# First layer of a graph kernel: one-hot comparisons that read the column numbers from a PSUM bank, and a sort whose ranks use one bank

## Chip, cores and metric

The kernel runs on one core of a Trainium2 chip. The metric is device time in microseconds of one execution. Before the change it is 9839.95 us, the median of three executions (9836.8 to 9844.66 us).

## What is computed

The reference runs two graph layers over 6,250 nodes with 128 features and 206,250 directed edges. Only the first layer and a sort for the second one matter here.

```python
msg = edge_weight[:, None] * x[src]                       # first layer
agg = segment_sum(msg, dst, num_segments=N)
out = relu((x + agg) @ W1 + b1) @ W2 + b2
x = layernorm(x + out)
# second layer, three hops: attention over the edges of each head
# (head = src), softmax per head, weighted sum of rel * agg[tail]
```

The second layer needs the edges grouped by `src`, the order in which it walks its heads. That sort depends on the indices alone, and the kernel does it while the first layer's gather runs.

## The kernel before

**The stage.** Edges are handled in tiles of 128 (one edge to a partition), four tiles to a group (`GROUP` = 4), and there are 1,664 tiles in 416 groups. All engines walk the same list of steps, each in a program order of its own, and meet at semaphores. Step i works on different groups in different functions; a "lag" says how many steps behind the newest group a function is. The stage is one block of the program (L1229 to L1251), in which each engine has one function that it calls at every step.

**First layer's part.** GpSimd (`pool_rows`, L602) issues one indirect DMA for each tile, which gathers 128 rows of `x` by their source index. The ring holds four groups of rows. ScalarE multiplies each tile by its edge weights (L1211) and copies the indices of later groups (L629). VectorE builds `hot`, a one-hot matrix for each tile, by comparing the row of numbers 0 to 127 (`column`, in SBUF) with each edge's target number (L1193). TensorE multiplies one by the other into bank 0 or 1 (L1223). VectorE then adds the result to `acc` (L1190).

**The sort's part.** A counting sort of the edges by source node rides along, with the same groups, in blocks of 32 groups (`IN_BLOCK`). VectorE makes two one-hots of each tile (`vector_tag`: `of_section` L1012, `of_low` L1014). TensorE sums them (`tensor_sum`, L1026 and L1028). 37 steps later (`RANK`) TensorE turns them into ranks (`tensor_rank`, L1095 and L1096, written to bank 4 or 5 in turn), and VectorE picks each edge's own rank (`vector_own` L1102, `vector_spot` L1110). 69 steps after the tag (`LAY`) the edges are laid out by two more one-hots: one on VectorE (`in_row` L1133, then two products `paid` L1141), one on ScalarE (`apart` L1152, `in_column` L1156). TensorE multiplies these two into bank 6 (`tensor_lay`, L1167). At a block's end there is extra work: `vector_totals`, `tensor_ahead`, `vector_carry`, a round trip through memory for the carries (SyncE, L1074 and L1078), and `vector_where`.

**Order within one step.** VectorE: add the group of three steps ago to `acc`, build `hot`, [`vector_where`], `own`, `in_row`, `spot`, `paid` twice, `of_section`, `of_low`, [totals, carry]. TensorE: L1223 for the group of two steps ago, rank, sum, [ahead], lay. ScalarE: weigh, copy indices, [laid], `apart` four times, `in_column`. GpSimd does nothing but issue gathers. The functions in brackets run once in 32 steps.

**What waits for what.** `hot` of step i waits for TensorE's L1223 of the same step i, since it has two buffers. `own` of step i stands behind it in VectorE's queue, and waits for the rank of TensorE's step i-1. In TensorE's step i the rank waits for `spot` of VectorE's step i-1:

```python
s.wait_ge((s_spot, done(lag + 2)))     # tensor_rank, L1094
```

Four of VectorE's operations at every step take `column` as one operand, and a second tensor in SBUF as the other: L1193, L1012, L1014 and L1133. `own` and the additions to `acc` take one operand from PSUM. `paid` takes both from SBUF.

Of the kernel before, what the change touches and what calls it, by code (L numbers as in the profile page):

```python
# [6 lines left out]
ALU = mybir.AluOpType  # L7
# [8 lines left out]
P = 128  # L16
BANK = 512
GROUP = BANK // P
# [102 lines left out]
def done(lag, per=1):  # L121
    return lambda i: per * (i - lag + 1) if i >= lag else 0
# [23 lines left out]
def phases(e, name, step, groups, total, rates, unroll=UNROLL):  # L146

    regs = {rate: e.alloc_register(f"{name}_rate{rate}") for rate in rates}
    spare = [e.alloc_register(f"{name}_until{n}") for n in range(8)]
    for start in range(0, total, IN_BLOCK):  # L150
        whole = start + IN_BLOCK <= total
        for i in range(start, start + 2 * unroll if whole else total):
            step(Step(e, i, groups))
        if whole:
            turns = IN_BLOCK // unroll - 2
            for rate in rates:
                e.reg_mov(regs[rate], rate)
            with e.Fori(0, turns) as turn:
                for b in range(unroll):
                    step(Step(e, start + 2 * unroll + b, groups, turn, regs, spare, unroll, turns))  # L160
                for rate in rates:
                    e.reg_add(regs[rate], regs[rate], rate)
    for r in [*regs.values(), *spare]:
        e.free_register(r)


def gnn_two_layers(nc, x, src, dst, edge_type, edge_weight, w1, b1, w2, b2, edge_emb, q_w, k_w, out):
# [3 lines left out]
    with top:  # L171
        def sem(name):
            return Sem(top.enter_context(nc.semaphore(name)))

        def tensor(ctx, name, shape, dt=F32):
            return ctx.enter_context(nc.sbuf_tensor(name, shape, dt))
# [5 lines left out]
        bank = [banks_used[:, i, :] for i in range(8)]  # L182
# [8 lines left out]
        H = P // 2  # L191
# [4 lines left out]
        column = tensor(top, "column", [P, P])  # L196
# [441 lines left out]
        S = z.sections  # L638
# [5 lines left out]
        with ExitStack() as ctx:  # L644
# [5 lines left out]
            above_half = tensor(ctx, "above_half", [P, P], BF16)  # L650
            ones_short = tensor(ctx, "ones_short", [P, P], BF16)
            two = tensor(ctx, "two", [2, P], BF16)
# [65 lines left out]
            with ExitStack() as tmp:  # L718
                start = tensor(tmp, "start", [H, 2])
# [241 lines left out]
            hot = tensor(inner, "l0_hot", [P, 2, GROUP, P])  # L961
# [3 lines left out]
            of_section = tensor(inner, "of_section", [P, IN * GROUP * S], BF16)  # L965
            of_low = tensor(inner, "of_low", [P, 2, GROUP, P], BF16)
            carry_rows = tensor(inner, "carry_rows", [2, IN * GROUP * S], BF16)
# [5 lines left out]
            own = tensor(inner, "own", [P, 2, GROUP, S])  # L973
# [5 lines left out]
            in_row = tensor(inner, "in_row", [P, GROUP, H], F16)  # L979
# [5 lines left out]
            s_carry, s_split, s_carried, s_rank, s_own, s_spot = (sem(f"sort_s_{n}") for n in ("carry", "split", "carried", "rank", "own", "spot"))  # L985
            s_where, s_in_row, s_paid, s_apart = (sem(f"sort_s_{n}") for n in ("where", "in_row", "paid", "apart"))
            s_in_column, s_laid, s_lain, s_blocks = (sem(f"sort_s_{n}") for n in ("in_column", "laid", "lain", "blocks"))
            s_carries = [sem(f"sort_s_carries{i}") for i in range(2)]
            b_totals, b_rank, b_laid, b_heads = 2, 4, 6, 7
            TAG, RANK, LAY = 0, IN_BLOCK + 5, IN + 5  # L990
            steps = z.sort_groups + LAY + 3
            paid_words = pay[:, :, :].bitcast(F16)
# [6 lines left out]
            def tagged(s, lag):  # L999
                return of_section[:, ring_at(s, lag, S)].rearrange("p (t s) -> p t s", s=S)  # L1000
# [6 lines left out]
            def vector_tag(s):  # L1007
                e = s.e
                if s.live(TAG, z.sort_groups):
                    cols = bass.ds(s.at(lambda i: GROUP * i), GROUP)  # L1010
                    s.wait_ge((s_summed, done(2)), (s_spot, done(IN)))
                    e.scalar_tensor_tensor(tagged(s, TAG), column[:, 0:S].unsqueeze(1).to_broadcast([P, GROUP, S]), 1.0,  # L1012
                                           sec_of[:, cols].unsqueeze(2).to_broadcast([P, GROUP, S]), ALU.mult, ALU.is_equal)
                    e.scalar_tensor_tensor(of_low[:, s.slot(TAG, 2), :, :], column[:, :].unsqueeze(1).to_broadcast([P, GROUP, P]), 1.0,  # L1014
                                           head_low[:, cols].unsqueeze(2).to_broadcast([P, GROUP, P]), ALU.mult, ALU.is_equal).then_inc(s_tagged.h, 1)

            def tensor_sum(s):
# [69 lines left out]
            def tensor_rank(s):  # L1087
                e, lag = s.e, RANK - 1
                if s.live(lag, z.sort_groups):
                    k, g2 = s.block(lag), s.slot(lag, 2)  # L1090
                    if s.begins_block(lag):
                        e.wait_ge(s_carries[k % 2].h, 16 * (k // 2 + 1))
                    s.wait_ge((s_spot, done(lag + 2)))
                    cols = ring_at(s, lag, S)  # L1094
                    e.matmul(bank[b_rank + g2][:, 0:GROUP * S], above_half[:, :], of_section[:, cols], start=True, stop=False)  # L1095
                    e.matmul(bank[b_rank + g2][:, 0:GROUP * S], two[:, :], carry_rows[:, cols], start=False, stop=True).then_inc(s_rank.h, 1)  # L1096

            def vector_own(s):
                if s.live(RANK, z.sort_groups):
                    g2 = s.slot(RANK, 2)  # L1100
                    s.wait_ge((s_rank, done(RANK)), (s_spot, done(RANK + 2)))
                    s.e.tensor_tensor(own[:, g2, :, :], bank[b_rank + g2][:, 0:GROUP * S].rearrange("p (t s) -> p t s", s=S), tagged(s, RANK), ALU.mult)\  # L1102
                        .then_inc(s_own.h, 1)

            def vector_spot(s):
# [24 lines left out]
            def vector_in_row(s):  # L1130
                if s.live(LAY, z.sort_groups):
                    s.wait_ge((s_paid, done(LAY + 1)))
                    s.e.scalar_tensor_tensor(in_row[:, :, :], column[:, 0:H].unsqueeze(1).to_broadcast([P, GROUP, H]), 1.0,  # L1133
                                             spot_row[:, ring_at(s, LAY)].unsqueeze(2).to_broadcast([P, GROUP, H]), ALU.mult, ALU.is_equal).then_inc(s_in_row.h, 1)

            def vector_paid(s):
# [44 lines left out]
            def vector_l0(s):  # L1181
                e = s.e
                if s.live(3):
                    q = load_sections(s, mybir.EngineType.DVE, at_wide, (z.sections - 1) * WIDE, 3)
                    s.wait_ge((s_acc, done(3)), (s_taken, lambda i: GROUP * (i - 3)))
                    for t in range(GROUP):
                        if t:
                            s.wait_ge((s_taken, lambda i, t=t: GROUP * (i - 3) + t))
                        to = acc[:, bass.ds(q[t], P)]
                        e.tensor_tensor(to, to, bank[s.slot(3, 2)][:, t * P:t * P + P], ALU.add).then_inc(s_taken.h, 1)  # L1190
                if s.live(0):
                    s.wait_ge((s_acc, done(2)))
                    e.scalar_tensor_tensor(hot[:, s.slot(0, 2), :, :], column[:, :].unsqueeze(1).to_broadcast([P, GROUP, P]), 1.0,  # L1193
                                           low_of[:, bass.ds(s.at(lambda i: GROUP * i), GROUP)].unsqueeze(2).to_broadcast([P, GROUP, P]),
                                           ALU.mult, ALU.is_equal).then_inc(s_l0_hot.h, 1)
                vector_where(s)
                vector_own(s)
                vector_in_row(s)
                vector_spot(s)
                vector_paid(s)  # L1200
                vector_tag(s)
                vector_totals(s)
                vector_carry(s)
# [26 lines left out]
            with nc.Block() as block:  # L1230
                @block.sync
                def _(e):
                    sync_sort(e)

                @block.gpsimd
                def _(e):
                    pool_rows(e, "l0", rows, idx, x, s_rt)

                @block.scalar
                def _(e):  # L1240
                    phases(e, "ga", scalar_l0, z.slot_groups, steps, (UNROLL, 16 * GROUP))

                @block.vector
                def _(e):
                    e.memset(counts[:, :], 0.0)
                    phases(e, "gv", vector_l0, z.slot_groups, steps, (UNROLL, GROUP * UNROLL))
                    e.wait_ge(s_taken.h, z.slot_tiles)

                @block.tensor
                def _(e):  # L1250
                    phases(e, "gt", tensor_l0, z.slot_groups, steps, (UNROLL, GROUP * UNROLL))  # L1251
# [674 lines left out]
```

## Time and profile before

| what | value |
|---|---|
| median of three executions | 9839.95 us |
| the profiled execution's own time | 9834.6 us |
| its span in the profile | 9832.9 us |
| busy: TensorE, VectorE, ScalarE, GpSimd | 7328.8, 6365.0, 5947.2, 6751.4 us |
| gathers of the first layer: number, busy | 1664, 1707.7 us |
| first and last of them start at | 346.9 and 2560.7 us |

Busy time is that of the instructions themselves. Times inside the profile are counted from the span's start. The stage that the diff touches lies between about 346 and 2788 us. The table's busy shares cover the whole kernel, so the stage has to be read by itself. GpSimd's instruction for a gather is the making of the DMA's descriptors; the transfer follows it.

### The profile page before, as it was taken

How to read it: one execution, taken by the hardware profiler on the slowest of the kernel's cores; microseconds unless marked ns; L12 is line 12 of the kernel's file. 1: busy time of each engine (PE TensorE's matmuls, PEld its weight loads, DVE VectorE, ACT ScalarE, POOL GpSimd, SP SyncE). 2: the span in 40 equal slices, each digit the busy share in tenths (PEclk: the TensorE clock that was granted, in tenths of full speed). 3: DMA queues.
4: the chain of work that ended last, by engine and by line, in shares of the span. 5: the costliest groups of instructions: out<-in, count | busy, mean ns of one | idle time of the engine just before them, and what ended most of it. 6: DMA issues, size and time to landing. Idle time of an engine off the chain costs nothing. (4 is left out here: it accounts for less than half of the span.)

```text
span 9832.9 us, 248228 instructions
## 1 busy us (share of the span) xinstructions
PE 7328.8 (75%) x47197; PEld 5463.0 (56%) x47197; DVE 6365.0 (65%) x27494; ACT 5947.2 (60%) x15127; POOL 6751.4 (69%) x6760
## 2 busy tenths in 40 slices
PE   0357777777749999999996777777776777777774
PEld 0345555555536777777764555555554555555553
DVE  2368877877656777777765666666665656666566
ACT  1137777777846666666664666666664666666663
POOL 0677777777327777777764777777774777777773
PEclk9657777777559999999998999999998999999997
DMA  1111211112217777777785666666665666666664
GB/s 45 40 50 50 51 50 50 51 50 50 22 35 213 222 224 222 223 224 223 223 209 140 176 175 176 176 175 176 175 176 124 173 174 174 175 173 174 172 175 103
DMA packets 1389939, 1398.93 MB, mean 142 GB/s; under 512 B 239111, under 2 KB 1066274, under 8 KB 1389602
## 3 DMA queue, kind: packets, MB, share of 16 engines
q1 hardware_dynamic: 1173096, 951.41, 31.9%
q0 software_dynamic: 215904, 443.45, 19.4%
q10 hardware_dynamic: 804, 2.56, 0.1%
q8 instruction: 50, 0.82, 0.0%
q14 instruction: 85, 0.70, 0.0%
HBM read 888.05 MB, written 183.75 MB: 109 GB/s over the span
## 5 line engine op out<-in xcount | busy, mean ns | idle before, releaser
L602 POOL DMA_INDIRECT tails<-node_rows,idx x4992 | 4925.2, 987 | 1866.6 <-issue 1516.0
L1655 DVE SCALAR_TENSOR_TENSOR acc<-acc,fade,banks 128x129 f32 x4992 | 1721.1, 345 | 1092.5 <-PE banks L1743 688.2
L602 POOL DMA_INDIRECT l_rows<-in_x_dram,l_idx x1664 | 1707.7, 1026 | 531.2 <-issue 500.9
L1743 PE MATMUL banks<-rt,weight_t 128*128 128x129 f32 x9984 | 1427.5, 286 | 804.4 <-DVE acc L1655 781.0
L1743 PEld LDWEIGHTS banks<-rt,weight_t 128*128 128x128 f32 x9984 | 1223.6, 192 | 1061.7 <-issue 1050.3
L1767 ACT ACTIVATE weight<-att,low 128x128 f32<-128x128 f32 x4992 | 1593.9, 395 | 344.5 <-DVE low L1694 342.1
L1751 ACT ACTIVATE weight_t<-banks 128x512 f32<-128x512 f32 x1248 | 746.3, 598 | 1570.2 <-PE banks L1730 1024.2
L1723 PE MATMUL banks<-right,window 128*128 128x128 f32 x9984 | 1391.0, 283 | 0.2 <-DVE tile_low L1661 0.2
L1661 DVE CUSTOM_DVE_ANT_0 att<-banks,mask 128x128 f32<-128x128 f32 x4992 | 1235.9, 285 | 103.6 <-PE banks L1723 100.5
L1734 PE MATMUL banks<-rtt,k_sb 128*128 128x512 f32 x2496 | 1288.1, 598 | 1.4 <-ACT rtt L1758 1.4
L1723 PEld LDWEIGHTS banks<-right,window 128*128 128x128 f32 x9984 | 1241.0, 195 | 28.2 <-DVE tile_low L1661 0.4
L1738 PEld LDWEIGHTS banks<-ident,rt 128*128 128x128 f32 x4992 | 569.5, 142 | 1175.4 <-DVE rt L1676 876.6
L1676 DVE SCALAR_TENSOR_TENSOR rt<-rel,tails 128x512 f32<-128x512 f32 x832 | 576.6, 693 | 967.8 <-DMA tails<-node_rows,idx 938.4
L1223 PE MATMUL banks<-l_weighed,l_hot 128*128 128x128 f32 x3328 | 723.0, 386 | 431.5 <-issue 399.2
L1738 PE MATMUL banks<-ident,rt 128*128 128x128 f32 x4992 | 795.1, 282 | 294.8 <-DVE rt L1676 284.2
L1754 ACT ACTIVATE right<-banks 128x512 f32<-128x512 f32 x1248 | 745.9, 598 | 343.6 <-PE banks L1734 295.0
L1223 PEld LDWEIGHTS banks<-l_weighed,l_hot 128*128 128x128 f32 x3328 | 628.4, 282 | 548.9 <-issue 533.2
L1211 ACT ACTIVATE l_weighed<-l_rows,l_weights 128x128 f32<-128x128 f32 x1664 | 531.5, 390 | 637.3 <-DMA l_rows<-in_x_dram,l_idx 637.3
L1758 ACT ACTIVATE rtt<-banks 128x512 f32<-128x512 f32 x1248 | 741.8, 594 | 277.3 <-PE banks L1738 270.3
L1167 PE MATMUL banks<-in_column,paid 128*64 128x256 f16 x3328 | 645.7, 360 | 268.6 <-ACT in_column L1156 221.7
L1730 PE MATMUL banks<-ident,weight 128*128 128x128 f32 x4992 | 761.2, 276 | 3.5 <-ACT weight L1767 2.4
L1152 ACT ACTIVATE apart<-spread,spot_left 128x256 f32<-128x256 f32 x1664 | 705.7, 494 | 18.7 <-DVE spot_left L1127 3.5
(293 smaller groups left out, 9300.8 us busy)
## 6 DMA issues: line engine op xcount, KB each, us to landing
window<-qt SPq DMA_DIRECT2D x4992, 64.0 KB
rel<-rel_kept SPq DMA_DIRECT2D x832, 256.0 KB
rows_in<-tile_rows SPq DMA_DIRECT2D x416, 256.0 KB
rel_kept<-rel SPq DMA_DIRECT2D x416, 256.0 KB
mask<-mask_kept SPq DMA_DIRECT2D x832, 128.0 KB
tails<-node_rows,idx POOLq DMA_INDIRECT x4992
mask_kept<-mask SPq DMA_DIRECT2D x416, 128.0 KB
l_rows<-in_x_dram,l_idx POOLq DMA_INDIRECT x1664
```

Source lines behind the costliest of these rows:

```text
L602: e.indirect_dma_start(out=rows[:, g, t % GROUP, :], out_offset=None, in_=of, in_offset=bass.IndirectOffsetOnAxis(ap=idx[:, b, t:t + 1], a ...
L1223: mm = s.e.matmul(bank[g2][:, t * P:t * P + P], hot[:, g2, t, :], weighed[:, g2, t, :], start=True, stop=True)
L1655: e.scalar_tensor_tensor(to, to, fade[:, g2, t:t + 1], bank[b_acc + t // 2][:, t % 2 * WIDE:t % 2 * WIDE + WIDE], ALU.mult, ALU.add).then_ ...
L1661: e.tensor_tensor_reduce(att[:, g2, t, :], bank[b_att][:, t * P:t * P + P], mask[:, g4, t, :], 1.0, START, ALU.add, ALU.min, tile_low[:, g ...
L1723: mm = e.matmul(bank[b_att][:, t * P:t * P + P], window[:, g4, t, :], right[:, g2, t * P:t * P + P], start=True, stop=True)
L1730: mm = e.transpose(bank[b_et][:, t * P:t * P + P], weight[:, g2, t, :], ident[:, :])
L1734: e.matmul(bank[b_kw][:, :], k_sb[:, :], rtt[:, s.slot(2, 2), :], start=True, stop=True).then_inc(s_kw.h, 1)
L1738: mm = e.transpose(bank[b_rtt][:, t * P:t * P + P], rt[:, s.slot(1, UNROLL), t, 0:z.D], ident[:, :])
L1743: mm = e.matmul(bank[b_acc + t // 2][:, t % 2 * WIDE:t % 2 * WIDE + WIDE], weight_t[:, s.slot(4, 2), t, :], rt[:, s.slot(4, UNROLL), t, :] ...
L1751: e.activation(weight_t[:, s.slot(4, 2), :, :].rearrange("p t d -> p (t d)"), bank[b_et][:, :], ACT.Copy).then_inc(s_ets.h, 1)
L1754: e.activation(right[:, s.slot(2, 2), :], bank[b_kw][:, :], ACT.Tanh).then_inc(s_th.h, 1)
L1767: e.activation(weight[:, g2, t, :], att[:, g2, t, :], ACT.Exp, scale=-1.0, bias=low[:, g4, t + 1:t + 2]).then_inc(s_exp.h, 1)
```

## The change

The diff does three things. It copies `column` once into bank 5 before VectorE's first step. It lets the four comparisons read it from there (`from_psum`). And, since bank 5 is taken, both ranks in turn now go to bank 4. TensorE's rank therefore waits until VectorE's `own` has read the rank before it, and no longer for `spot`.

```diff
+            s_column = sem("sort_s_column")
-            b_totals, b_rank, b_laid, b_heads = 2, 4, 6, 7
+            b_totals, b_rank, b_column, b_laid, b_heads = 2, 4, 5, 6, 7
+            from_psum = bank[b_column][:, 0:P]
...
-                    e.scalar_tensor_tensor(tagged(s, TAG), column[:, 0:S].unsqueeze(1).to_broadcast([P, GROUP, S]), 1.0,
+                    e.scalar_tensor_tensor(tagged(s, TAG), from_psum[:, 0:S].unsqueeze(1).to_broadcast([P, GROUP, S]), 1.0,
...
-                    e.scalar_tensor_tensor(of_low[:, s.slot(TAG, 2), :, :], column[:, :].unsqueeze(1).to_broadcast([P, GROUP, P]), 1.0,
+                    e.scalar_tensor_tensor(of_low[:, s.slot(TAG, 2), :, :], from_psum.unsqueeze(1).to_broadcast([P, GROUP, P]), 1.0,
...
-                    s.wait_ge((s_spot, done(lag + 2)))
+                    s.wait_ge((s_own, done(lag + 1)))
                     cols = ring_at(s, lag, S)
-                    e.matmul(bank[b_rank + g2][:, 0:GROUP * S], above_half[:, :], of_section[:, cols], start=True, stop=False)
-                    e.matmul(bank[b_rank + g2][:, 0:GROUP * S], two[:, :], carry_rows[:, cols], start=False, stop=True).then_inc(s_rank.h, 1)
+                    e.matmul(bank[b_rank][:, 0:GROUP * S], above_half[:, :], of_section[:, cols], start=True, stop=False)
+                    e.matmul(bank[b_rank][:, 0:GROUP * S], two[:, :], carry_rows[:, cols], start=False, stop=True).then_inc(s_rank.h, 1)
...
-                    s.e.scalar_tensor_tensor(in_row[:, :, :], column[:, 0:H].unsqueeze(1).to_broadcast([P, GROUP, H]), 1.0,
+                    s.e.scalar_tensor_tensor(in_row[:, :, :], from_psum[:, 0:H].unsqueeze(1).to_broadcast([P, GROUP, H]), 1.0,
...
-                    e.scalar_tensor_tensor(hot[:, s.slot(0, 2), :, :], column[:, :].unsqueeze(1).to_broadcast([P, GROUP, P]), 1.0,
+                    e.scalar_tensor_tensor(hot[:, s.slot(0, 2), :, :], from_psum.unsqueeze(1).to_broadcast([P, GROUP, P]), 1.0,
...
                     e.memset(counts[:, :], 0.0)
+                    e.tensor_copy(from_psum, column[:, :]).then_inc(s_column.h, 1)
+                    e.wait_ge(s_column.h, 1)
```

## Rows read from the trace of the kernel before

**Rows 1.** The page's costliest groups: the first layer's gathers; busy, mean ns, idle before.

```profile
L602 POOL DMA_INDIRECT l_rows<-in_x_dram,l_idx x1664 | 1707.7, 1026 | 531.2 <-issue 500.9
```

**Rows 2.** Line L602 by itself: duration ns min/median/max, first and last start us.

```profile
L602 POOL DMA_INDIRECT l_rows<-in_x_dram,l_idx x1664: 941/947/1511, 346.9 to 2560.7; - x185
```

**Rows 3.** Timeline of VectorE and GpSimd: start us, us, engine, operation, idle before.

```profile
1508.74 1.54 DVE L1190 TENSOR_TENSOR acc<-acc,banks 128x128 f32 x4
...
1509.35 0.95 POOL L602 DMA_INDIRECT l_rows<-in_x_dram,l_idx  x1 [0.30 <-issue]
...
1511.70 0.69 DVE L1193 SCALAR_TENSOR_TENSOR l_hot<-column,l_low_of 128x512 f32<-128x512 f32 x1 [1.42 <-PE banks L1223]
...
1511.85 1.36 POOL L602 DMA_INDIRECT l_rows<-in_x_dram,l_idx  x1 [0.31 <-issue]
```

**Rows 4.** Windows: busy us and count by engine, TensorE's granted clock, DMA share, GB/s.

```profile
347.00:716.00 369.00, 182.00 (x1170) 154.07 (x1170) 203.94 (x561) 93.91 (x306) 284.59 (x277) 0.50 0.20 50
716.00:2565.00 1849.00, 1341.05 (x9014) 1017.53 (x9015) 1472.32 (x4282) 1447.54 (x3297) 1423.03 (x1387) 0.72 0.21 50
1278.60:1295.60 17.00, 14.48 (x79) 10.72 (x80) 12.21 (x35) 12.37 (x29) 13.04 (x14) 0.52 0.19 48
1346.90:1360.40 13.50, 6.45 (x60) 4.98 (x61) 11.81 (x36) 9.63 (x23) 10.45 (x11) 0.98 0.17 45
```

**Rows 5.** VectorE's groups by form, 716 to 2565 us: busy, mean ns, idle before.

```profile
L1193 DVE SCALAR_TENSOR_TENSOR l_hot<-column,l_low_of 128x512 f32<-128x512 f32 x346 | 239.8, 693 | 227.4 <-PE banks L1223 224.5 <-issue 1.4
...
L1102 DVE TENSOR_TENSOR own<-banks,of_section 128x196 f32<-128x196 f32 x346 | 122.4, 354 | 0.4
L1012 DVE SCALAR_TENSOR_TENSOR of_section<-column,sec_of 128x196 f32 x263 | 92.5, 352 | 0.0
```

**Rows 6.** Timeline of a step at half clock, TensorE and VectorE together.

```profile
1284.50 2.04 PE L1223 MATMUL banks<-l_weighed,l_hot 128*128 128x128 f32 x8 [1.18 <-issue]
1286.34 0.37 PE L1095 MATMUL banks<-of_section,above_half 128*128 x1
...
1286.70 0.69 DVE L1193 SCALAR_TENSOR_TENSOR l_hot<-column,l_low_of 128x512 f32<-128x512 f32 x1 [1.39 <-PE banks L1223]
...
1286.92 0.22 PE L1026 MATMUL banks<-of_section,picker 128*128 x1
...
1287.31 0.35 DVE L1102 TENSOR_TENSOR own<-banks,of_section 128x196 f32<-128x196 f32 x1
```

**Rows 7.** The rest of a step at half clock: sum, lay, and the next step's L1223.

```profile
1218.18 0.22 PE L1026 MATMUL banks<-of_section,picker 128*128 128x49 bf16 x1
...
1218.63 1.92 PE L1167 MATMUL banks<-in_column,paid 128*64 128x256 f16 x8
...
1220.47 2.08 PE L1223 MATMUL banks<-l_weighed,l_hot 128*128 128x128 f32 x8
```

**Rows 8.** Timeline of steps at full clock, TensorE and VectorE together.

```profile
1211.25 0.20 PE L1026 MATMUL banks<-of_section,picker 128*128 128x49 bf16 x1
...
1211.56 1.06 PE L1167 MATMUL banks<-in_column,paid 128*64 128x256 f16 x8
...
1354.53 1.13 PE L1223 MATMUL banks<-l_weighed,l_hot 128*128 128x128 f32 x8 [1.16 <-issue]
...
1355.50 0.25 PE L1095 MATMUL banks<-of_section,above_half 128*128 x1
...
1355.82 0.69 DVE L1193 SCALAR_TENSOR_TENSOR l_hot<-column,l_low_of 128x512 f32<-128x512 f32 x1 [0.51 <-PE banks L1223]
1355.87 0.20 PE L1026 MATMUL banks<-of_section,picker 128*128 x1
```

**Rows 9.** VectorE's timeline: two starts of L1193 with no idle time between.

```profile
1213.82 0.68 DVE L1193 SCALAR_TENSOR_TENSOR l_hot<-column,l_low_of 128x512 f32<-128x512 f32 x1
...
1218.29 0.68 DVE L1193 SCALAR_TENSOR_TENSOR l_hot<-column,l_low_of 128x512 f32<-128x512 f32 x1
```

**Rows 10.** Waits, 722 to 2480 us: us in total, times, longest us.

```profile
PE banks L1045 <- DVE totals L1037: 27.4, 10, 3.3
```

More of the change, by code:

```diff
@@ L1089, in tensor_rank @@
                 if s.live(lag, z.sort_groups):
-                    k, g2 = s.block(lag), s.slot(lag, 2)
+                    k = s.block(lag)
                     if s.begins_block(lag):
                         e.wait_ge(s_carries[k % 2].h, 16 * (k // 2 + 1))
-                    s.wait_ge((s_spot, done(lag + 2)))
+                    s.wait_ge((s_own, done(lag + 1)))
                     cols = ring_at(s, lag, S)
-                    e.matmul(bank[b_rank + g2][:, 0:GROUP * S], above_half[:, :], of_section[:, cols], start=True, stop=False)
-                    e.matmul(bank[b_rank + g2][:, 0:GROUP * S], two[:, :], carry_rows[:, cols], start=False, stop=True).then_inc(s_rank.h, 1)
+                    e.matmul(bank[b_rank][:, 0:GROUP * S], above_half[:, :], of_section[:, cols], start=True, stop=False)
+                    e.matmul(bank[b_rank][:, 0:GROUP * S], two[:, :], carry_rows[:, cols], start=False, stop=True).then_inc(s_rank.h, 1)
             def vector_own(s):
@@ L1101, in vector_own @@
                     s.wait_ge((s_rank, done(RANK)), (s_spot, done(RANK + 2)))
-                    s.e.tensor_tensor(own[:, g2, :, :], bank[b_rank + g2][:, 0:GROUP * S].rearrange("p (t s) -> p t s", s=S), tagged(s, RANK), ALU.mult)\
+                    s.e.tensor_tensor(own[:, g2, :, :], bank[b_rank][:, 0:GROUP * S].rearrange("p (t s) -> p t s", s=S), tagged(s, RANK), ALU.mult)\
                         .then_inc(s_own.h, 1)
```

## The prediction

> **What bounds the kernel now.** The page comes first. The stage of the diff has 1,664 gathers, and GpSimd is busy 1707.7 us with them and idle 531.2 us, nearly all of it put down to "issue" and not to a wait for another engine [rows 1]. Line L602 by itself gives the pace: the first starts at 346.9 us, the last at 2560.7 us, so 2213.8 / 1663 = 1.331 us from one to the next [rows 2]. The timeline shows 0.30 us between two gathers each time [rows 3], and 1.026 + 0.305 makes up that 1.331. So GpSimd never waits for data. It sets the stage's length, with 4 x 1.331 = 5.325 us per step of four tiles.
>
> The median gather takes 947 ns and the mean 1026, with a maximum of 1511 [rows 1, 2]. The timeline says what the long ones have in common. The gather that starts at 1511.85 does so inside a `hot` that ends at 1512.39, and takes 1.36 us: 0.41 more than usual, where 0.54 of `hot` was left. The gather that starts at 1509.35 does so inside the additions to `acc`, which read one operand from PSUM, and takes 0.95 [rows 3]. I read it so: a VectorE operation with both operands in SBUF holds up a gather that starts under it. All long gathers together cost 1664 x (1.026 - 0.947) = 131 us.
>
> Who is second? TensorE's granted clock is 0.50 until 716 us, where L1167 has not begun, and 0.72 on average after that, changing between half and full (1.2 and 2.4 GHz) [rows 4]. In a stretch at half clock TensorE is busy 14.48 of 17.0 us; in one at full clock 6.45 of 13.5 us [rows 4]. VectorE is idle 227.4 us before `hot`, nearly all of it waiting for L1223 [rows 5].
>
> **Part 1, four comparisons read PSUM.** What it frees lies on the bound. If all long gathers became 0.947 us, a step would be 4 x (0.947 + 0.305) = 5.01 us. `paid` keeps both operands in SBUF, and so keeps a tenth or so of the 131 us (it holds 0.75 us of a step, the four comparisons about 2 us). I take 5.04 us per step as GpSimd's floor. Over 415 steps 5.325 - 5.04 is worth 118 us; the bounds are 0 (the reading of the rows is wrong) and 131.
>
> The price of a PSUM operand on VectorE: `own` reads PSUM and takes 354 ns for 196 elements, `of_section` reads SBUF alone and takes 352 for as many [rows 5]. That is 2 ns, 8 ns for four in a step; I take zero. A gain is excluded, since the pair shows none at equal size. What no row shows is an operand in PSUM that is repeated four times over. From L1012 to L1193, 316 more elements cost 341 ns, so the 196 of `own` cost 211 of its 354 and the other 143 are fixed [rows 5]. Were each repeat to pay that anew, `hot` would take 3 x 0.143 = 0.43 us more; that is the bound from above. The Trainium skill, VectorE: DVE Perf Modes, "The TRN2 errata", gives VectorE 58 fixed cycles from SBUF and 120 from PSUM. By that page each comparison would take 62 cycles or some 65 ns more, an estimate, and a step's VectorE work 0.26 us more. The two rows show 2 ns where that page has 65.
>
> The one copy of `column` and its wait come before VectorE's first step. The nearest row is `own`, 0.35 us for more elements [rows 5]; it costs 0 to 0.4 us, and I take 0, as TensorE and ScalarE have nothing to do without the first gather.
>
> **Part 2, one bank for the ranks.** No instruction is added, but TensorE waits in a new place. In step i its rank must wait for `own` of VectorE's step i. `own` stands behind `hot`, and `hot` waits for L1223 of that same step. Before, rank followed L1223 at once (1286.34 after 1284.50) [rows 6]. Behind the waiting rank stand sum, lay and the next L1223. So one loop now runs through both engines, and its length per step is, at half clock:
> - L1223's start to `hot`'s start 2.20 (1284.50 to 1286.70); to `own`'s start 0.61 and its end 0.35; handing over about 0.06, an estimate (L1193 starts 0.16 behind L1223's end) [rows 6].
> - rank to sum 0.58 (1286.34 to 1286.92) [rows 6]; sum to lay 0.45, lay to the next L1223 1.84 [rows 7].
> - Sum 6.09 us, over today's 5.325.
>
> At full clock: 1.29 to `hot` [rows 8], 0.96 and 0.06 as before, rank to sum 0.37, sum to lay 0.31, lay about 1.03 [rows 8]; 4.02 us. But VectorE itself needs 4.47 us from one `hot` to the next [rows 9], so such a step takes 4.47.
>
> The rows ring (four groups) lets GpSimd run on while TensorE is late, so the mean counts. Of the time 0.56 is at half clock (0.72 = 1 - 0.56/2). If whole steps fall at one clock, a step takes 1 / (0.56/6.09 + 0.44/4.47) = 5.26 us. If clock changes fall evenly within steps, VectorE's limit is not felt: 1.18 us of a step do not scale (0.61 + 0.35 + 0.06 + 0.16), 2.84 us at full clock do and take 4.91 at half, so in the mix 2.84 / (0.44 + 0.56 x 2.84/4.91) = 3.71, in all 4.89 us. A block's end adds TensorE's wait for the totals, 27.4 us in 10 blocks [rows 10], or 0.09 us per step, and extra work on VectorE that I put at as much again, an estimate: up to 0.18. That makes 4.89 to 5.44. With GpSimd's floor of 5.04 beside a loop of almost the same length, I take 5.25.
>
> **The sum.** Until L1167 begins the loop is shorter even at half clock (6.09 less lay's 1.84 is 4.25), so GpSimd bounds: 69 steps x (5.35 - 5.01) = 23 us, where 369/69 = 5.35 is what they take now [rows 4]. After that 346 steps x (5.33 - 5.25) = 28 us. Together -51 us. Against the profiled execution's 9834.6 us that is 9784; the median of the runs is 5 us above it, so I say 9788.
>
> **Rivals.**
> - **The loop hides.** Slow and fast steps even out in the ring, and GpSimd's floor holds: 346 x 0.29 + 23 = 123 us, 9717. For: the even mix gives 4.89. Against: VectorE's 4.47 and the blocks' ends. Chance 0.17.
> - **The loop binds and TensorE sits at half clock longer.** TensorE's clock stayed at half through a stretch in which it was busy 14.48 of 17.0 us [rows 4], and the new wait (0.61 + 0.35 + 0.06 us and more, after each L1223) makes it idle more. At a share of 0.68, whole steps take 1 / (0.68/6.09 + 0.32/4.47) = 5.46, with 0.15 for blocks 5.61: 346 x 0.28 - 23 = +74 us, 9914. It turns to slower where a step passes 5.33 + 23/346 = 5.40 us, that is a share of 0.56 if whole steps fall at one clock, and about 0.64 halfway between the two ways of mixing. Chance 0.26, likeliest near +45.
> - **They cancel.** A step of 5.35 to 5.45: within 20 us. Chance 0.15.
> - **GpSimd is not freed.** The Trainium skill, SBUF — State Buffer, "Who interferes with whom", infers that an operation with two SBUF inputs takes only the shared read interface, and that making descriptors needs the write one. As a mechanism here: the long gathers stay as they are, and only part 2 is left; a step stays at 5.325 or becomes the loop's, 9840 to 9880. Against it stand the 1.36 us gather and the 0.95 one [rows 3]. Chance 0.04, counted as slower.
>
> **How the numbers follow.** About 0.2% (20 us) is what a measurement of this kernel can tell from no change. My forecast (a gain of 20 to 90 us) has 0.38, the full gain 0.17: faster 0.55. Same 0.15. Slower 0.26 + 0.04 = 0.30. The range runs from 9716 (the full gain) to 9900 (most of the slower cases). The forecast's own range is 9750 to 9820.
>
> **What the profile would show.** Part 1 right: L602 `l_rows` has a mean of 950 to 965 ns, and gathers that start under `hot` take 0.95; `hot` and `of_low` stay near 690. If they stay at 1026, part 1 is wrong. Part 2 right: a new wait of TensorE's L1095 for VectorE's `own` of about a microsecond per step, hundreds of us in all, and GpSimd begins to wait for ScalarE's indices in parts of the stage. If that wait is there and GpSimd still never waits, the first rival holds. A granted clock under 0.68 in the stage goes with the second. The forecast is wrong if the last gather starts before 2470 us or after 2541.

## The result, and the profile after

The changed kernel takes 9953.57 us (median of four executions, 9946.97 to 9965.68) against 9842.27 us for the kernel before in the same session. The ratio is 1.0115, with a 95% interval of 1.0098 to 1.0133. A gain was forecast, and a loss came, beyond the range given, which ended at 9900 us. The profiled execution took 9951.03 us, 116 us more than that of the kernel before.

Two groups of the page, and line L602 by itself (its columns are those of [rows 1] and [rows 2]), changed kernel:

```profile
span 9949.4 us, 248229 instructions
...
L602 POOL DMA_INDIRECT l_rows<-in_x_dram,l_idx x1664 | 1588.5, 955 | 743.8 <-issue 493.0
...
L1225 PE MATMUL banks<-l_weighed,l_hot 128*128 128x128 f32 x3328 | 772.7, 405 | 115.1 <-issue 93.0
```

```profile
L602 POOL DMA_INDIRECT tails<-node_rows,idx x4992: 942/947/1462, 3055.6 to 9828.8; - x200
L602 POOL DMA_INDIRECT l_rows<-in_x_dram,l_idx x1664: 941/947/1206, 349.3 to 2656.8; - x185
```

The first part of the change did all that it was meant to. The gathers' mean fell from 1026 to 955 ns [rows 1], and the longest from 1511 to 1206 [rows 2]. GpSimd is busy 119 us less. Yet the last gather starts at 2656.8 us instead of 2560.7, 96 us later: GpSimd's idle time grew by 213 us. From its first gather to its last the stage takes 94 us more (2307.5 us against 2213.8), and the gathers begin 2 us later. Of the other 20 us, 19 lie in the second layer, whose code is the same (see the end of the experiments).

The windows before and after L1169 (L1167 before) begins, with the columns of [rows 4], changed kernel:

```profile
349.00:696.00 347.00, 188.19 (x1160) 157.10 (x1160) 203.46 (x561) 93.93 (x306) 262.27 (x278) 0.50 0.21 53
696.00:2667.00 1971.00, 1502.94 (x9018) 1121.23 (x9018) 1463.13 (x4282) 1435.06 (x3306) 1326.24 (x1387) 0.68 0.20 47
```

The first 69 steps now take 347 us and took 369 [rows 4], 22 us less. The other 346 take 1971 and took 1849: 5.70 us a step against 5.34. The granted clock fell from 0.72 to 0.68. The waits of the stretch from 722 to 2480 us, with the columns of [rows 10], changed kernel:

```profile
ACT apart L1154 <- PE banks L1169: 408.6, 267, 3.2
PE banks L1097 <- DVE own L1104: 400.8, 308, 2.8
...
POOL l_rows L602 <- issue: 365.1, 1131, 2.1
DVE l_hot L1195 <- PE banks L1225: 323.9, 255, 2.8
POOL l_rows L602 <- ACT l_idx L629: 207.3, 108, 6.0
```

TensorE's rank (L1097) waits 400.8 us for `own`, 1.3 us each time. Behind that, ScalarE waits for TensorE's lay (L1169), and GpSimd waits for the indices that ScalarE copies (L629). GpSimd no longer sets the pace. A step at half clock, from the timeline of the changed kernel:

```profile
1282.94 0.69 DVE L1195 SCALAR_TENSOR_TENSOR l_hot<-banks,l_low_of 128x512 f32<-128x512 f32 x1 [1.47 <-PE banks L1225]
1283.55 0.35 DVE L1104 TENSOR_TENSOR own<-banks,of_section 128x196 f32<-128x196 f32 x1
...
1284.06 0.34 PE L1097 MATMUL banks<-of_section,above_half 128*128 x1 [1.27 <-DVE own L1104]
...
1284.61 0.22 PE L1028 MATMUL banks<-of_section,picker 128*128 x1
...
1285.24 1.89 PE L1169 MATMUL banks<-in_column,paid 128*64 128x256 f16 x8
...
1287.06 1.67 PE L1225 MATMUL banks<-l_weighed,l_hot 128*128 128x128 f32 x8
```

The reader sees the loop in one piece: `hot` waits for TensorE, `own` stands behind `hot`, the rank waits for `own`, and sum, lay and the next L1225 stand behind the rank. `hot` itself takes 0.69 us, as it did from SBUF [rows 3].

### The profile page after: what moved, and what is told of

It is laid out like the page before. It is cut to its first block and busy times, and to the rows that moved or that the text cites. A ratio compares the mean times of both kernels' runs of the same rounds, so it can differ in the third digit from the quotient of the medians.

```text
span 9949.4 us, 248229 instructions
## 1 busy us (share of the span) xinstructions
PE 7485.5 (75%) x47197; PEld 5548.4 (56%) x47197; DVE 6355.9 (64%) x27495; ACT 5933.8 (60%) x15127; POOL 6650.4 (67%) x6760
## 5 line engine op out<-in xcount | busy, mean ns | idle before, releaser
L602 POOL DMA_INDIRECT tails<-node_rows,idx x4992 | 4942.1, 990 | 1868.4 <-issue 1521.2
L602 POOL DMA_INDIRECT l_rows<-in_x_dram,l_idx x1664 | 1588.5, 955 | 743.8 <-issue 493.0
L1225 PE MATMUL banks<-l_weighed,l_hot 128*128 128x128 f32 x3328 | 772.7, 405 | 115.1 <-issue 93.0
L1225 PEld LDWEIGHTS banks<-l_weighed,l_hot 128*128 128x128 f32 x3328 | 667.4, 298 | 238.3 <-issue 238.2
L1169 PE MATMUL banks<-in_column,paid 128*64 128x256 f16 x3328 | 671.6, 370 | 57.0 <-ACT in_column L1158 44.7
```

What stands on the lines that cost most here:

```text
L602: e.indirect_dma_start(out=rows[:, g, t % GROUP, :], out_offset=None, in_=of, in_offset=bass.IndirectOffsetOnAxis(ap=idx[:, b, t:t + 1], a ...
L1225: mm = s.e.matmul(bank[g2][:, t * P:t * P + P], hot[:, g2, t, :], weighed[:, g2, t, :], start=True, stop=True)
```

## Experiments

The kernel before was run beside each group of kernels, on the same chip. Its own median differs by up to 0.9% from group to group (9753.88 to 9842.27 us), so ratios are compared. The times in the expectations of e1 to e4 were written with the kernel before at 9840 us; beside them it took 9797, so they are to be read some 43 us lower.

| run | what differs | median us | before us | ratio, 95% interval |
|---|---|---|---|---|
| changed kernel | | 9953.57 | 9842.27 | 1.0115 [1.0098, 1.0133] |
| e1 | part 2 alone | 9934.27 | 9797.25 | 1.0140 [1.0123, 1.0157] |
| e2 | part 1 alone | 9693.18 | 9797.25 | 0.9893 [0.9876, 0.9909] |
| e3 | changed, `own` ahead of `hot` | 9690.19 | 9797.25 | 0.9890 [0.9873, 0.9906] |
| e4 | changed, rank at the step's end | 9692.32 | 9797.25 | 0.9894 [0.9877, 0.9910] |
| e5 | changed, wait filled with 10 matmuls | 9710.00 | 9820.39 | 0.9890 [0.9874, 0.9907] |
| e6 | e3, `hot` from SBUF | 9749.86 | 9820.39 | 0.9928 [0.9912, 0.9945] |
| e7 | changed kernel again | 9935.15 | 9820.39 | 1.0116 [1.0100, 1.0133] |
| e8 | kernel before again | 9822.10 | 9820.39 | 1.0003 [0.9992, 1.0013] |
| e9 | changed, wait filled with 4 matmuls | 9683.41 | 9753.88 | 0.9924 [0.9907, 0.9940] |
| e10 | before, with the 10 matmuls | 9774.72 | 9753.88 | 1.0021 [1.0011, 1.0030] |

**The two parts, each alone.** e1 keeps the one bank and its wait and takes the column numbers from SBUF:

```diff
-            from_psum = bank[b_column][:, 0:P]
+            from_psum = column[:, :]
...
-                    e.tensor_copy(from_psum, column[:, :]).then_inc(s_column.h, 1)
-                    e.wait_ge(s_column.h, 1)
```

> Part 2 alone: ranks in one bank with the wait for own, column still read from SBUF. Theory A (the new wait closes a loop L1223-hot-own-rank-sum-lay through TensorE and VectorE, and that loop sets the step): about as slow as the changed kernel or somewhat slower, since the first 69 steps no longer gain 23 us and hot is still lengthened now and then by gathers: 9950 to 9985 us, the gathers' mean stays at 1.02 us or so, TensorE's L1097-type wait for own 400 us or more. Theory B (reading the column numbers from PSUM is what costs): 9840, as before. Theory C (the two parts cost about half each): 9890 to 9910.

e2 keeps the two banks and their old wait. The bank for the column numbers is bank 7, whose head counts move to a corner of the totals' banks:

```diff
-                        mm = e.matmul(bank[b_heads][:, 0:S], of_low[:, s.slot(lag, 2), t, :], own_column,
-                                      start=begins and k == 0 and t == 0, stop=True, skip_group_check=True)
+                        mm = e.matmul(bank[b_totals + k % 2][:, 4 * H:4 * H + S], of_low[:, s.slot(lag, 2), t, :], own_column,
+                                      start=False, stop=True, skip_group_check=True)
...
+                    e.tensor_tensor(head_counts[:, :], head_counts[:, :], bank[b_totals + k % 2][:, 4 * H:4 * H + S], ALU.add)
                     e.tensor_copy(totals[:, :], bank[b_totals + k % 2][:, 0:S]).then_inc(s_totals.h, 1)
```

> Part 1 alone: the column numbers in a bank of their own, ranks in two banks with the old wait. The bank comes from the head counts, which are summed in a corner of the totals' banks and added up once in 32 steps (one small VectorE operation, 13 in all). Theory A: the gathers' mean falls to 0.955 us, GpSimd stays the bound, a step takes 5.04 to 5.10 us in place of 5.33, so 9720 to 9750 us. Theory B: 9930 or more. Theory C: 9880 to 9900.

Part 2 alone costs 1.40% and part 1 alone gains 1.07%. The page's line of the gathers, first e1, then e2:

```profile
L602 POOL DMA_INDIRECT l_rows<-in_x_dram,l_idx x1664 | 1678.6, 1009 | 686.2 <-issue 492.8
```

```profile
L602 POOL DMA_INDIRECT l_rows<-in_x_dram,l_idx x1664 | 1590.5, 956 | 530.9 <-issue 505.2
```

In e1 the gathers stay long and GpSimd idles as well. In e2 they are short, and its idle time is what it was before, 531 us [rows 1]. Against the kernel before, e1 loses 137 us and e2 gains 104 us. So the loss comes with the new wait, and none of it from reading PSUM. Theory A holds in both, theories B and C fall. As the loop sets the pace with either kind of gather, the changed kernel keeps little of part 1: 1.15% against 1.40%, which is about the 22 us of the first 69 steps.

**The wait without the loop.** e3 moves one call of VectorE. `own` needs the rank of TensorE's step before, and nothing of this step's L1225:

```diff
                         e.tensor_tensor(to, to, bank[s.slot(3, 2)][:, t * P:t * P + P], ALU.add).then_inc(s_taken.h, 1)
+                vector_own(s)
                 if s.live(0):
                     s.wait_ge((s_acc, done(2)))
...
                 vector_where(s)
-                vector_own(s)
                 vector_in_row(s)
```

> The changed kernel with one call moved: VectorE does own ahead of hot, so that own no longer stands behind the wait for L1223 of the same step. One bank for the ranks and the column numbers from PSUM stay. Theory A: the loop is cut, TensorE's wait for own almost vanishes, GpSimd bounds again: 9715 to 9760 us, granted clock in the stage back to 0.72 or so. Theory B: no change from the changed kernel, 9950. A rival of its own: one bank costs by itself, since rank and own now alternate strictly wherever they stand: 9850 to 9950.

e4 leaves VectorE alone and moves TensorE's rank:

```diff
-                tensor_rank(s)
                 tensor_sum(s)
                 tensor_ahead(s)
                 tensor_lay(s)
+                tensor_rank(s)
```

> The changed kernel with TensorE's rank moved from behind L1223 to the end of its step, behind lay. The wait for own stays as it is, but sum and lay now run while VectorE does hot and own. Theory A: the wait is covered, 9715 to 9780 us. If the wait is only moved (own late even at the step's end, above all at full clock), 9800 to 9900. Theory B: 9950.

Both keep one bank and the new wait, and both are 1.1% faster than the kernel before and 2.2% faster than the changed one. Two of the waits of e3, from 720 to 2400 us:

```profile
POOL l_rows L602 <- issue: 403.8, 1325, 0.3
...
PE banks L1097 <- DVE own L1104: 216.9, 184, 3.8
```

That TensorE's wait for `own` would almost vanish was a miss: 216.9 us of it are left. But GpSimd's longest idle stretch is 0.3 us: the wait costs nothing, as it is no longer part of a loop longer than GpSimd's step. The rival that one bank costs by itself falls.

**How much is the clock's?** e5 puts matmuls that nobody reads into the wait:

```diff
+                if s.live(RANK - 1, z.sort_groups):
+                    for n in range(10):
+                        s.e.matmul(bank[b_heads][:, 2 * P:3 * P], before[:, :], ones_short[:, :], start=False, stop=True, skip_group_check=True)
                 tensor_rank(s)
```

> The changed kernel with ten extra 128-column bf16 matmuls in each of TensorE's steps, between L1223's group and the wait of the rank, into a corner of bank 7 that nothing reads: work that fills the wait of about 1.3 us. Theory A2 (a good part of the loss is that the wait lets the granted clock drop, which then lengthens the loop itself): the granted clock in the stage rises from 0.68 to over 0.85, the step falls towards GpSimd's 5.07 us, and the kernel becomes faster by adding work, 60 to 230 us below the changed kernel. Rival (the wait alone counts, and the clock hardly): the clock rises but the time stays within 30 us of the changed kernel's, or grows where the extra matmuls outlast the wait.

The timeline of e5, TensorE and one row of VectorE, full clock:

```profile
1285.01 0.72 PE L1229 MATMUL banks<-ones_short,before 128*128 128x128 bf16 x10
1286.43 0.26 PE L1097 MATMUL banks<-of_section,above_half 128*128 x1 [0.70 <-DVE own L1104]
...
1286.81 0.20 PE L1028 MATMUL banks<-of_section,picker 128*128 x1
...
1287.50 1.03 PE L1169 MATMUL banks<-in_column,paid 128*64 128x256 f16 x8
```

```profile
1285.94 0.35 DVE L1104 TENSOR_TENSOR own<-banks,of_section 128x196 f32<-128x196 f32 x1
```

The windows from 720 to 2400 us, with the columns of [rows 4]. The changed kernel:

```profile
720.00:2400.00 1680.00, 1281.27 (x7671) 955.95 (x7669) 1244.87 (x3645) 1218.57 (x2808) 1133.20 (x1185) 0.68 0.19 47
```

e8, the kernel before:

```profile
720.00:2400.00 1680.00, 1216.78 (x8246) 925.18 (x8246) 1347.08 (x3917) 1324.41 (x3017) 1294.44 (x1266) 0.73 0.20 51
```

e3:

```profile
720.00:2400.00 1680.00, 1297.75 (x8666) 977.45 (x8665) 1419.61 (x4114) 1389.19 (x3164) 1275.31 (x1329) 0.78 0.21 53
```

e5:

```profile
720.00:2400.00 1680.00, 1316.25 (x12072) 1042.80 (x12072) 1412.27 (x4146) 1397.55 (x3187) 1272.54 (x1338) 0.94 0.21 53
```

e9, with four matmuls (below):

```profile
720.00:2400.00 1680.00, 1279.58 (x9938) 984.06 (x9936) 1390.43 (x4095) 1379.19 (x3156) 1269.73 (x1326) 0.86 0.19 53
```

e10, the kernel before with the ten (below):

```profile
720.00:2400.00 1680.00, 1201.47 (x11473) 999.27 (x11474) 1354.27 (x3941) 1330.53 (x3031) 1292.37 (x1273) 0.89 0.18 51
```

The last count of a row, GpSimd's, is the number of gathers in 1680 us: 1185 in the changed kernel, 1266 before, 1338 in e5, although e5 keeps the whole loop and adds ten matmuls to each step. The granted clock is 0.94 and was 0.68. Rank, sum and lay wait for `own` as before, but at full clock that loop is shorter than GpSimd's step: between 720 and 2400 us GpSimd never idles longer than 0.31 us here. The gain of 2.2% over the changed kernel lies at the upper end of what theory A2 expected. So the loop is what makes the stage depend on TensorE's clock, and the low clock is what makes the loop longer than a gather's pace. In these runs either alone costs nothing.

e9 has four in place of ten.

> The changed kernel with four extra matmuls per step in the wait in place of ten, about 0.4 us of work at half clock in a wait of 1.3 us. Theory A2 (the loss is carried by the clock): a granted clock between 0.69 and 0.94 and a time between the two kernels, 9730 to 9900 us with the kernel before near 9820. Rival (something else in the ten matmuls helped, or it is all or nothing): the time of the changed kernel (1.2% over before) or that of the ten (1.1% under before).

Four suffice for a clock of 0.86 and a ratio of 0.9924, between the changed kernel and e5, and nearer to e5. e10 gives the ten to the kernel before, where GpSimd bounds.

> The kernel before (two banks, column numbers in SBUF) with the ten extra matmuls at the same place. Theory A2: the granted clock in the stage rises from 0.73 to 0.9 or more, and the time stays within 15 us, since GpSimd's gathers set the pace and not TensorE. Rival (a higher clock is worth time by itself in this stage, whatever bounds it): 30 us or more faster.

There the clock is 0.89, where e8 has 0.73, and the gathers stay at about their pace (1273 against e8's 1266). GpSimd's idle time ahead of its gathers is 530.6 us here and 531.0 in e8. So a higher clock alone gained nothing where TensorE is not in the bounding loop. The whole time rose by 0.21%, 21 us, where 15 at most were expected. Where it rose is open: e8, the profile of the kernel before that stands beside it here, is from another chip, on which that kernel takes 66 us more.

**The gathers' delay, one operation of four.** e6 is e3 with `hot` alone back on SBUF:

```diff
-                    e.scalar_tensor_tensor(hot[:, s.slot(0, 2), :, :], from_psum.unsqueeze(1).to_broadcast([P, GROUP, P]), 1.0,
+                    e.scalar_tensor_tensor(hot[:, s.slot(0, 2), :, :], column[:, :].unsqueeze(1).to_broadcast([P, GROUP, P]), 1.0,
```

> The kernel with own ahead of hot, with hot alone reading the column numbers from SBUF again; the other three comparisons stay on PSUM. Theory D (a gather that starts under a VectorE operation with two SBUF operands waits for its end): the gathers' long ones come back where they start under hot and nowhere else new, about 40 to 60 us in all, mean 0.98 us, and the kernel is 30 to 60 us slower than with own first alone. Rival (the whole gain needs all four, or comes from elsewhere): no change, or all 115 us.

Line L602 by itself, first e3, then e6:

```profile
L602 POOL DMA_INDIRECT l_rows<-in_x_dram,l_idx x1664: 938/944/1212, 343.3 to 2442.4; - x185
```

```profile
L602 POOL DMA_INDIRECT l_rows<-in_x_dram,l_idx x1664: 940/944/1460, 350.4 to 2487.7; - x185
```

The stage from first to last gather takes 2137.3 us against 2099.1: 38 us for one operation of the four. The gathers' mean is 980 ns against 957, and 1664 x 0.023 is 38 us as well. Counted from the traces by the VectorE operation under which a gather starts, 213 of the 239 gathers under `hot` take over 1 us in e6, and none of 238 in e3. The long ones under `paid` fall from 129 to 10, so 38 us is what is left of a larger delay under `hot`. So the delay follows the operation that has two operands in SBUF, and its cost reaches the end in full where GpSimd bounds. The two runs are from different chips, but their ratios agree: 0.9928 - 0.9890 is 0.38%, or 37 us.

**Again on one chip.**

> The changed kernel as it is, beside the kernel before on the same chip. First profile: the stage took 97 us more and the second layer, whose code is the same, 19 us more. If the 19 us are a matter of one execution or chip, the second layer takes what it takes in the others of this chip (within 8 us) and the ratio is 1.010 to 1.013; if the change does it, it is again 15 to 20 us longer than in the kernel before.

> The kernel before as it is, for a profile from the same chip as the others: a stage of 2,214 us from the first gather to the last, a granted clock of 0.72 in it, and the second layer within 8 us of that of the changed kernel in this call.

The ratio of e7 repeats the first, 1.0116. The second layer's gathers, first e7, then e8:

```profile
L602 POOL DMA_INDIRECT tails<-node_rows,idx x4992: 938/944/1466, 3049.9 to 9808.9; - x200
```

```profile
L602 POOL DMA_INDIRECT tails<-node_rows,idx x4992: 938/944/1464, 2955.5 to 9695.8; - x200
```

From first to last it is 6759.0 us in the changed kernel and 6740.3 in the one before, 19 us more. In the first pair of profiles it was 6773.2 and 6754.5, also 19. So it was not a matter of one execution or chip, and what e8 expected of the second layer (within 8 us) was a miss. Its instructions are the same. The page's line of the same gathers, first e7, then e8:

```profile
L602 POOL DMA_INDIRECT tails<-node_rows,idx x4992 | 4926.4, 987 | 1870.0 <-issue 1513.0
```

```profile
L602 POOL DMA_INDIRECT tails<-node_rows,idx x4992 | 4909.2, 983 | 1868.4 <-issue 1511.8
```

So 17 of the 19 us are longer gathers. Counted from the traces, they are those that start under `rt`, a VectorE operation with two operands in SBUF: 693 gathers in e7 against 647 in e8, with means of 1247 and 1244 ns, where the median gather takes 944. It is the same delay, met more often. On e7's chip, e5 has 6755.4 from first to last and e6 6738.1. What moves the gathers under `rt` is open, and it is a sixth of the loss.

## Why the prediction was wrong

- **What bounds the kernel: right.** GpSimd's gathers did, and the reading of their long ones as VectorE operations with two SBUF operands is shown by e2, e3 and e6. The floor was put at 5.04 us a step. e3's later steps, the 346 after the first 69, take 5.08 (from the starts of `hot`).
- **Part 1's price: right.** `hot` 691 ns on average against 693 [rows 5], `of_section` 354 against 352 (lines below). The estimate by the Trainium skill, VectorE: DVE Perf Modes, "The TRN2 errata", some 65 ns more each, is not seen here. The inference of the Trainium skill, SBUF — State Buffer, "Who interferes with whom", by which the gathers would have stayed long, is contradicted on one chip: with the comparisons reading SBUF (e1) the gathers' mean is 1009 ns, with PSUM (e2) it is 956.
- **The first 69 steps: right.** 23 us were expected, 22 came.
- **Part 2 at half clock: right.** 6.09 us were worked out. Counted from the trace, there are 97 steps between 720 and 2440 us that lie wholly at half clock, and they take 6.22 on average: 3.31 to the rank, 0.55 to the sum, 0.55 to lay and 1.82 to the next step. The difference is the handing over from `own`, 0.15 us (median) in place of 0.06, and sum to lay, where 0.45 was put in.
- **The mean step: this is the step that failed.** It was put at 5.25 us, and is 5.70. "If whole steps fall at one clock" gave 5.26 and "if clock changes fall evenly within steps" gave 4.89, both with the share of half clock of the kernel before, 0.56. Three things were wrong, and a middle between the two ways could not hold them.
  - The share of half clock rose to 0.64 (a granted clock of 0.68). Put into the first way, that alone gives 5.39 us.
  - Neither way of mixing is what happens. Among 299 steps counted, one lay wholly at full clock; it took 4.02 us, the loop's own sum and not VectorE's 4.47, which shows in e9 (median 4.49 of 175 such steps). 201 are mixed and take 5.49, although the clock is full for over half of their time, where the even way gives about 4.7. In these steps the granted clock is 0.76 from L1225's start to the rank, 0.92 to the sum, 0.91 to lay, and 0.69 from lay to the next L1225. Over L1225's own matmuls it is 0.60 in all steps: the full clock falls mostly on the wait and on rank and sum, and least on the longest pieces. From L1225's start to the rank is 3.05 us in the mixed steps, where half clock has 3.31 and full clock 2.35. L1225's mean rose to 405 ns from 386 (line below). A share of time was used as a share of work.
  - The sum after the rank was priced too low. Sum to lay takes 0.62 us on average over the 299 steps, and 0.66 in the mixed ones, where 0.45 and 0.31 were put in for half and full clock; that makes up about 0.2 of the 0.45 us that the mean step was off. 0.05 of it are the block ends, nine steps in which lay comes some 2 us behind the sum. Most of the rest is that at full clock the four pairs of the sum start 0.15 us apart (median of 170 sums), where the kernel before has 0.055 (median of 180).

The first pairs of a sum at full clock, changed kernel:

```profile
1290.38 0.19 PE L1028 MATMUL banks<-of_section,picker 128*128 x1
...
1290.54 0.20 PE L1028 MATMUL banks<-of_section,picker 128*128 x1
```

The kernel before, the pair behind the one at 1355.87 [rows 8], and the page's line of L1223:

```profile
1355.93 0.18 PE L1026 MATMUL banks<-of_section,picker 128*128 x1
```

```profile
L1223 PE MATMUL banks<-l_weighed,l_hot 128*128 128x128 f32 x3328 | 723.0, 386 | 431.5 <-issue 399.2
```

VectorE's groups of the changed kernel, with the window and columns of [rows 5]:

```profile
L1195 DVE SCALAR_TENSOR_TENSOR l_hot<-banks,l_low_of 128x512 f32<-128x512 f32 x324 | 223.8, 691 | 337.5 <-PE banks L1225 337.3
...
L1014 DVE SCALAR_TENSOR_TENSOR of_section<-banks,sec_of 128x196 f32 x244 | 86.3, 354 | 0.0
```

- **The rivals.** The second one named the place, the mechanism and the direction. It put the share of half clock at 0.68 and the step at 5.61 us; 0.64 and 5.70 came, and its 74 us stand beside 94 measured in the stage. That it came so close is partly luck: with 0.64 its own sum gives 5.39 + 0.15 = 5.54. It had 0.26. The point from which it decides (5.40 us a step) was right; what was wrong was to take a step beyond that point as unlikely. "GpSimd is not freed", "the loop hides" and "they cancel" fell.

## What to carry to other kernels

Before a buffer is given up, write down the loop that its new wait closes, engine by engine, with all that stands ahead of the releasing instruction in its queue: the wait here was for a short operation (0.35 us) that stood behind a wait for TensorE. A move of one call in either engine's order took the loop apart and turned 1.2% lost into 1.1% gained. Where a loop runs through TensorE and its clock changes within a step, a mean by the share of time can be far too short (4.7 us against 5.49 here); a loop that fits under the bound at half clock leaves no room for that error, though no run here tries such a one. And where GpSimd's gathers set the pace, look at which VectorE operations have two operands in SBUF when they start.

## What the runs showed of the hardware

- A gather that starts under a VectorE operation with both operands in SBUF takes up to 1.5 us and not 0.95, and ends 0.82 us behind the end of that operation (median of the long ones; [rows 3] has 1513.21 against 1512.39). One that starts under an operation with one of them in PSUM takes 0.95. In the changed kernel `paid` is the only operation of every step with both in SBUF: all 100 gathers over 1 us start under it, and the mean is 955 ns.
- Ten matmuls a step that nobody reads made the changed kernel 2.2% faster (1.0116 to 0.9890 on one chip), by a granted clock of 0.94 in place of 0.68. In the kernel before, whose pace GpSimd sets, the same matmuls gave nothing (1.0021).
- At full clock the four pairs of matmuls of the sum start 0.15 us apart in the changed kernel and 0.055 in the kernel before. The wait ahead of the rank is not enough to explain it: in the kernel before, five sums at full clock whose rank waited over 0.3 us still have 0.055, and in e3, 99 whose rank did not wait so long have a median of 0.12. The cause is open.
